# Linear attention whose weights and state are multiplied first, a Gram over 255 columns and ones, and another order of the drain and the late stage

## The chip, the cores and the metric

The kernel runs on one core of one Trainium2 chip. The metric is the device time in microseconds of one execution of the whole program. "Before" is the kernel as given, "after" is the changed one.

## The reference, cut to what matters

Four residual stages follow one another on x of 8 batches x 512 rows x 256 columns; `ln` is a layernorm over the 256 columns without gain or bias. The change is in the third, the attention without softmax:

```
x = x + ln(softmax_attention(ln(x)))          # 16 heads of 64, causal, with a slope bias
x = x + ln(linear_layer(ln(x)))
z  = ln(x)                                    # third stage
q  = z + z @ Wq + bq
k_i = z + z @ Wk[i] + bk[i]   (i = 0, 1)
v_i = z + z @ Wv[i] + bv[i]
state = prod_i (k_i^T v_i / 1024), per head of 16 columns
x = x + ln( (ln(q @ state) * ln_g + ln_b) @ Wo + bo )
x = x + ln( shared_ffn(ln(x)) + top8_of_64_experts(ln(x)) )
```

Neither kernel forms k and v. With the Gram matrix G = z^T z the state is A_k^T G A_v with A = I + W, and terms for the biases.

## The kernel before, in words

The five engines have one hand-ordered program each, coupled by semaphores. The program has four stretches.

**Attention stage** (about 0 to 1190 us of the trace). A batch is eight *steps*, one for each pair of heads; step g runs the scores of pair g and the transposes and value product of pair g-1. Batches 1 to 6 run in a loop, batch 0 ahead of it and batch 7 behind it. Steps run in the order 1 to 7, then 0. What TensorE does in a step is the tuple `TENSOR_STEP`: `P0`, `P1` are the two projections of the next pair (L1541), `S0`, `S1`, `S2` the three thirds of the scores (L1552), `Tsu` the transposes of the probabilities of head s, third u (L1564), `O` the value product (L1578). ScalarE's is `SCALAR_STEP` (`Esk` and `Fsk` are pieces of the exponentials, L798; `T`, `P`, `O` copy PSUM out, L781), VectorE's is `VECTOR_STEP` (`R0`, `R1`, `L2` add the bias and take the row minimum, L1081; `J` are reciprocals, L1090). GpSimd multiplies each head's probabilities by the reciprocals, four instructions a head (L675), and T00 waits for it.

The letters `b`, `q`, `k`, `e` (`A`, `B`, `C` on VectorE) are slots. The tables `TENSOR_AT`, `SCALAR_AT`, `VECTOR_AT`, `X_AT` and `RING_AT` put into a slot of a step the work of the *previous* batch p (everything behind its softmax attention), the norm of the following batch, and the value projections `V` 0 to 7 (L1532). Two PSUM banks, 4 and 5, form a ring through which P, V, T and O results pass in the order of issue; the ring's other users are `X`, `L` and, before only, `Q`.

Batch p's linear attention is a chain of parts: `x2_norm` writes z into `xn`; `gram` (L1630) forms G, with two extra columns of ones for the column sums; `L` (L1611) transposes z into `xTp`; `t1` (L1638) is G A_v; `state` is A_k^T t1 (L1646) and the sums' product with A_v (L1653); VectorE adds the bias terms and multiplies the two states into `sbd`, blocks of 16 on the diagonal; `Q` (L1616) forms the queries `qTp` from `xTp`; `rows` (L1661) multiplies them by `sbd`. Then follow `l1_sum`, `l1_norm`, `l1o_T`, `l1wo` (L1588) and so on.

**Drain and chain** (1180 to 1400 us). `drain` ends batch 7's softmax attention; `last_leave` (L1758) is its output projection over heads, into banks WO_BANK and WO_BANK + 1. It begins with

```
                pe.wait_ge(ring_ready, ring_count(a, ("O", HP - 2)))
                pe.wait_ge(biased, at(i, H * T, H * T))
                last_leave(range(HP - 2))
```

Batch 7's later parts then stand between *units* of the shared feed-forward of batches 0 to 4, in the order of the list `CHAIN` (`shared_hidden`, L1854, and every seventh unit `shared_out`, L1866).

**Experts** (1400 to 2064 us), L1951 and L1964. The change does not touch them.

**Late stage** (2064 us to the end). The shared feed-forward of batches 5 to 7 (n = 0, 1, 2), six hidden units f each, and meanwhile on VectorE the final norms of all batches. `shared_hidden` of unit f waits until VectorE's `gate` (L1364) of unit f-2 is done. `FINISH_AT` says behind which gate (n, f) VectorE does `sums` (statistics, L1004) and `scaled` (before: an inverse square root by eight small instructions, L1016 to L1031, and then the scaling, L1463) of which batch.

Of the kernel before, what the change touches and what calls it, by code (L numbers as in the profile page):

```python
# [39 lines left out]
ATT_STEPS, POST_STEPS = 17, 164  # L40
# [39 lines left out]
def bass_sandwich(nc, x, wq, wk, wv, wo, bo, ffn_w, ffn_d, l1_wq, l1_wqT, l1_bq, l1_wk, l1_bk, l1_wv, l1_bv,  # L80
# [12 lines left out]
    with ctx:  # L93
# [140 lines left out]
        gram_psum, gram_ready, ssum_ready = sem("gram_psum"), sem("gram_ready"), sem("ssum_ready")  # L234
# [47 lines left out]
        def score_banks(hp, u):  # L282
# [6 lines left out]
        TENSOR_AT = {(2, 'e'): ('ffn_T',), (3, 'q'): ('ffn',), (4, 'k'): ('gram',), (4, 'e'): ('t1',), (5,  # L289
                   'b'): ('state',), (6, 'q'): ('rows',), (7, 'b'): ('l1o_T',), (7, 'q'): ('l1wo',), (0,  # L290
                   'k'): ('moe_T',), (0, 'e'): ('logits',)}
        SCALAR_AT = {(2, 'e'): ('ffn_T',), (4, 'k'): ('gram',), (7, 'q'): ('l1o_T',), (0, 'k'): ('moe_T',), (0,
                   'e'): ('gates',)}
        VECTOR_AT = {(1, 'A'): ('wo_norm',), (1, 'B'): ('x1_sum',), (2, 'C'): ('x1_norm',), (3, 'B'): ('ffn_sum',
# [3 lines left out]
        X_AT = {(4, 'A'): 'means', (5, 'A'): 'rsqrt', (6, 'A'): 'scale'}  # L298


        RING_AT = {(1, 'b'): (('V', 4),), (2, 'q'): (('V', 5),), (4, 'b'): (('V', 6),), (4, 'q'): (('V', 7),), (5,
                   'b'): (('L', 0), ('L', 1)), (5, 'k'): (('Q', 0), ('Q', 1)), (6, 'k'): (('X', 0),), (7, 'b'): (('X',
                   1),), (7, 'e'): (('V', 0), ('V', 1)), (0, 'b'): (('V', 2),), (0, 'e'): (('V', 3),)}
# [105 lines left out]
        def t_unit(a, n):  # L409
# [7 lines left out]
                   'unit', 'unit', 'x1_sum', 'x1_norm', 'unit', 'unit', 'ffn_T', 'ffn', 'ffn_sum', 'ffn_norm', 'unit',  # L417
                   'x2_sum', 'x2_norm', 'unit', 'unit', 'gram', 'l1_T', 'unit', 't1', 'qp', 'unit', 'unit', 'state',
                   'unit', 'rows', 'l1_sum', 'l1_norm', 'unit', 'unit', 'l1o_T', 'unit', 'l1wo', 'unit', 'l1o_sum',
                   'unit', 'unit', 'l1o_norm', 'unit', 'unit', 'x3_sum', 'x3_norm', 'moe_T', 'logits', 'gates1',  # L420
                   'gates', 'gates2', 'unit', 'unit', 'rank', 'slots', 'unit', 'unit', 'unit']
# [1621 lines left out]
```

## Time and profile before

| | |
|---|---|
| median of 3 runs | 2169.01 us (2167.77 to 2172.38) |
| profiled execution, own time | 2168.89 us |
| profiled execution, span | 2166.8 us |
| TensorE busy | 2102.9 us, 97% |
| TensorE idle behind GpSimd's normalising | 27.1 us in 17 waits |
| chain that ended last | TensorE 83%, VectorE 7% |

The span is what the trace covers, 2.1 us less than the execution's own time. Busy time of TensorE is the union of its matmuls; each f32 matmul of the program appears as two instructions. "Idle before" is how long the engine stood still ahead of a group and which engine's instruction ended that.

### The profile page before, as it was taken

The numbers are of one execution on the slowest core, as the hardware profiler recorded it, in microseconds if no ns is written. First come the engines' busy times: TensorE is split into PE (matmuls) and PEld (weight loads), VectorE is DVE, ScalarE is ACT, GpSimd is POOL, SyncE is SP. The second block draws the span as 40 slices with busy tenths as digits, with TensorE's granted clock in tenths as the row PEclk, the third lists the DMA queues.
The fourth block names the chain that finished last, engine by engine and source line by source line (L and its number), as shares of the span: only waits on it lengthen the run. The fifth ranks groups of instructions, "written<-read, shape, count | busy, mean of one in ns | idle before, by whom it ended". The sixth has DMA issues, their size and how long they took to land.

```text
span 2166.8 us, 37485 instructions
## 1 busy us (share of the span) xinstructions
PE 2102.9 (97%) x11844; PEld 1550.7 (72%) x11844; DVE 975.6 (45%) x3780; ACT 828.7 (38%) x2130; POOL 842.5 (39%) x958
## 2 busy tenths in 40 slices
PE   8999999999999999999998999999999999999998
PEld 4555656566556656656565665799999999999956
DVE  3426655655565565575565534122222222222246
ACT  4746545645645555465465212111111111111110
POOL 3426526626446356266266230413232223222222
PEclk9999999999999999999999999999999999999999
DMA  9400001000000000000001300278778777888841
GB/s 319 121 0 11 11 22 64 35 30 25 25 18 21 35 16 5 31 17 6 20 22 58 139 28 35 70 264 270 257 259 272 269 260 257 268 262 270 270 109 59
DMA packets 101979, 245.43 MB, mean 113 GB/s; under 512 B 22916, under 2 KB 78435, under 8 KB 93488
## 3 DMA queue, kind: packets, MB, share of 16 engines
q1 hardware_dynamic: 75696, 223.83, 28.6%
q0 software_dynamic: 26112, 19.55, 5.5%
q8 instruction: 80, 1.31, 0.3%
q14 instruction: 91, 0.75, 0.1%
HBM read 193.71 MB, written 87.91 MB: 130 GB/s over the span
## 4 chain that ended last, share of the span: by engine, by line
PE 83%; DVE 7%; issue 4%; ACT 2%; POOL 2%; DMA 1%; DVEq 0%; POOLq 0%; ACTq 0%
PE bank L1951 19%; PE bank L1964 9%; PE bank L1541 9%; PE bank L1588 7%; PE bank L1854 6%; PE bank L1564 6%; PE bank L1578 5%; PE bank L1552 5%; PE bank L1866 3%; PE bank L1532 3%; POOL prob L675 2%; DVE stats L1004 2%; PE bank L1638 1%; PE bank L1616 1%; PE bank L1630 1%
## 5 line engine op out<-in xcount | busy, mean ns | idle before, releaser
L675 POOL TENSOR_TENSOR prob<-prob,rsum 128x128 f32<-128x128 f32 (+3 forms) x512 | 349.5, 715 | 541.6 <-DVE rsum L1090 541.5
L1951 PE MATMUL bank<-pT,big_w 128*128 128x160 f32 x3072 | 438.2, 299 | 0.0
L1951 PEld LDWEIGHTS bank<-pT,big_w 128*128 128x128 f32 x3072 | 422.7, 190 | 0.1
L680 POOL DMA_INDIRECT disp<-send,slot x288 | 285.4, 991 | 198.1 <-DVE slot L1284 109.5
L798 ACT ACTIVATE prob<-prob,negmax 128x512 f32<-128x512 f32 (+3 forms) x512 | 287.3, 568 | 80.6 <-DVE negmax L1081 80.1
L726 POOL DMA_INDIRECT acc<-qk,token_e x64 | 99.1, 1549 | 490.1 <-issue 171.4
L1081 DVE CUSTOM_DVE_ANT_0 prob<-bank,bias 128x512 f32<-128x512 f32 (+3 forms) x512 | 220.7, 487 | 109.7 <-PE bank L1552 100.5
L1541 PE MATMUL bank<-xT,big_w 128*128 128x512 f32 x512 | 250.9, 614 | 6.4 <-ACT v_s L781 3.5
L956 ACT ACTIVATE pT<-bank 128x480 f32<-128x480 f32 x128 | 73.1, 571 | 458.7 <-PE bank L1951 458.7
L1410 DVE TENSOR_TENSOR pT<-pT,bank 128x480 f32<-128x480 f32 x128 | 83.8, 655 | 335.9 <-PE bank L1951 335.8
L1964 PE MATMUL bank<-pT,big_w 128*128 128x160 f32 x1536 | 219.3, 299 | 0.0
L781 ACT ACTIVATE pT<-bank 128x512 f32<-128x512 f32 (+1 forms) x384 | 182.6, 538 | 90.5 <-PE bank L1564 90.3
L1564 PEld LDWEIGHTS bank<-ident,prob 128*128 128x128 f32 x1280 | 145.3, 142 | 99.4 <-issue 60.8
L1964 PEld LDWEIGHTS bank<-pT,big_w 128*128 128x128 f32 x1536 | 210.6, 190 | 0.0
L1564 PE MATMUL bank<-ident,prob 128*128 128x128 f32 x1280 | 177.6, 278 | 27.9 <-POOL prob L675 27.1
L1552 PE MATMUL bank<-qk 64*128 64x512 f32 (+3 forms) x1024 | 173.2, 456 | 0.0
L1552 PEld LDWEIGHTS bank<-qk 64*128 64x128 f32 x1024 | 87.9, 186 | 106.6 <-issue 85.2
L1541 PEld LDWEIGHTS bank<-xT,big_w 128*128 128x128 f32 x512 | 91.2, 193 | 94.1 <-issue 81.0
L1578 PE MATMUL bank<-pT,v_s 128*64 128x512 f32 (+3 forms) x1024 | 152.0, 439 | 0.7 <-ACT pT L781 0.6
L781 ACT ACTIVATE v_s<-bank 128x512 f32<-128x512 f32 x74 | 44.2, 597 | 253.3 <-PE bank L1532 194.0
L1532 PE MATMUL bank<-big_w,xT 128*128 128x512 f32 x256 | 121.5, 608 | 0.1
L1578 PEld LDWEIGHTS bank<-pT,v_s 128*64 128x64 f32 x1024 | 65.4, 136 | 75.5 <-issue 62.9
(197 smaller groups left out, 2501.5 us busy)
## 6 DMA issues: line engine op xcount, KB each, us to landing
big_w<-ew SPq DMA_DIRECT2D x64, 1536.0 KB, 6.9
big_w<-ew SPq DMA_DIRECT2D x64, 768.0 KB, 5.9
disp<-send SPq DMA_DIRECT2D x1, 10272.0 KB, 37.4
xT<-disp SPq DMA_DIRECT2D x64, 160.5 KB, 5.4
disp<-send,slot POOLq DMA_INDIRECT x288
x<-x SPq DMA_DIRECT2D x8, 512.0 KB, 4.0
x_d<-x SPq DMA_DIRECT2D x8, 512.0 KB, 2.7
hT_d<-hT SPq DMA_DIRECT2D x8, 512.0 KB, 2.6
```

What stands on the lines that cost most here:

```text
L675: i = g.tensor_tensor(pr, pr, rsum[:, n, t:t + 1].to_broadcast([P, COLS[t]]), ALU.mult)
L680: g.indirect_dma_start(out=disp, out_offset=bass.IndirectOffsetOnAxis(ap=slot[:, t, k:k + 1], axis=0), in_=send[:, t, :], in_offset=None, ...
L781: return a.activation(dst, src, ACT.Copy)
L798: a.activation(prob[:, n % 4, at_t], prob[:, n % 4, at_t], ACT.Exp, bias=negmax[:, n, t:t + 1], scale=-1.0, accum_out=psumm[:, n, t:t + 1] ...
L1081: v.tensor_tensor_reduce(out=prob[:, n % 4, P_AT[t]:P_AT[t] + COLS[t]], in0=bank[score_banks(hp, u)[s]][:, col:col + COLS[t]], in1=bias[:, ...
L1532: ins = mm(ring_bank(a, key)[:], xT[:, c, m % T * P:(m % T + 1) * P], wv_s[:, c, m // T * 512:(m // T + 1) * 512], start=(c == 0), stop=(c ...
L1541: ins = mm(ring_bank(a, key)[:], w[:, c, hp * P:(hp + 1) * P], xT[:, c], start=(c == 0), stop=(c == C - 1))
L1552: ins = mm(bank[score_banks(hp, u)[s]][:, col:col + COLS[t]], qT[half, hp % 2, t * P:(t + 1) * P], kT[half, hp % 2, 0:COLS[t]], start=True ...
L1564: ins = nc.tensor.transpose(ring_bank(a, key)[:, col + (t - j) * P:col + (t - j + 1) * P], prob[:, n % 4, P_AT[t] + j * P:P_AT[t] + (j + 1 ...
L1578: ins = mm(dst[s * DH:(s + 1) * DH, j * P:N], v_s[:, j, (2 * hp + s) * DH:(2 * hp + s + 1) * DH], pT[:, s, T_AT[j]:T_AT[j] + N - j * P], s ...
L1951: i = mm(bank[2 * half + 1 - part][:, q * CAP:(q + 1) * CAP], w1[:, c, f * P:(f + 1) * P], xbT[:, c], start=(c == 0), stop=(c == C - 1), s ...
L1964: i = mm(bank[(4, 7)[c]][:, 0:CAP], w2[:, f, c * P:(c + 1) * P], act_e[:, f], start=(f == 0), stop=(f == FC - 1), skip_group_check=True)
```

## The change

1. **Order of the products.** The `Q` units, `qTp`, and the product of the sums with A_v are gone. A new part `fuse` multiplies A_q (loaded transposed) by `sbd` into a 256 x 256 matrix `fused`, ScalarE copies it out, and `rows` multiplies `xTp` by it.
2. **255 columns and ones.** The rows of z sum to zero, so column 0 is dropped: the Gram, the transposes and A_q read `xn` from column 1 on, and column 256, which holds ones, takes its place. The biases become the last row or column of the A matrices (more, smaller DMAs at the start, and some subtractions once in batch 0 on VectorE). The bias terms on VectorE in `t1` and `state` fall away; ScalarE copies `t1` out instead.
3. **Drain.** `WO_BANK` is 0 instead of 2, the wait is for all but the last two bias results, and in batch 7's step 7 VectorE does the last third of the last pair ahead of `x3_norm`.
4. **Orders.** All slot tables, `TENSOR_STEP`, `SCALAR_STEP`, `CHAIN` and `FINISH_AT` are new, and the inverse root is a part of its own, `roots`.

```
-        WO_BANK = 2
+        WO_BANK = 0
-            return RING_BANKS[0] if (i[1], f) == (0, 1) else 2 * (f % 2)
+            return RING_BANKS[0] if (i[1], f) == (0, 1) else 2 * ((f + (i[1] < EARLY)) % 2)
-        TENSOR_STEP = ('b', 'P0', 'S0', 'S1', 'q', 'T00', 'P1', 'T01', 'T02', 'T10', 'T11', 'S2', 'T12', 'k', 'O', 'e')
-        SCALAR_STEP = ('b', 'F03', 'F13', 'P0', 'q', 'E00', 'T00', 'E01', 'P1', 'T01', 'T02', 'T10', 'T11', 'E02', 'T12',
-                       'E10', 'E11', 'k', 'O', 'e', 'E12')
+        TENSOR_STEP = ('P0', 'b', 'S0', 'S1', 'q', 'T00', 'P1', 'T01', 'T02', 'T10', 'T11', 'k', 'T12', 'S2', 'O', 'e')
+        SCALAR_STEP = ('F03', 'F13', 'P0', 'b', 'q', 'E00', 'T00', 'E01', 'P1', 'T01', 'T02', 'T10', 'T11', 'k', 'E02',
+                       'E10', 'T12', 'E11', 'E12', 'O', 'e')
...
-                     (1, 0): [("scaled", 1)], (1, 1): [("sums", EARLY)], (1, 2): [("scaled", EARLY)],
+        FINISH_AT = {(0, 5): [("sums", 0), ("roots", 0)], (1, 0): [("scaled", 0), ("sums", 1)],
...
-                    for c in range(C):
-                        a.activation(ssum_b[:, c], ones_f[:], ACT.Copy,
-                                     scale=gram[:, c, D:D + 1]).then_inc(ssum_ready, 1)
+                elif part == "t1":
+                    for k in range(KS):
+                        act.wait_ge(t1_psum, at(p, KS, k + 1))
+                        a_copy(t1[:, k].rearrange("p c d -> p (c d)"), bank[PA + k][:]).then_inc(t1_ready, 1)
+                elif part == "fuse":
+                    act.wait_ge(fused_psum, at(p, 1, 1))
+                    a_copy(fused[:].rearrange("p c d -> p (c d)"), bank[PB][:]).then_inc(fused_ready, 1)
...
+                    if part == "B" and a[0] is None and a[1] == B - 1 and g == HP - 1:
+                        last_pair()
...
-                            ins = mm(bank[PA + c][:, 0:D + 2], xn[:, t, c * P:(c + 1) * P], xn[:, t, 0:D + 2],
+                            ins = mm(bank[PA + c][:, 0:D], xn[:, t, c * P + 1:(c + 1) * P + 1], xn[:, t, 1:D + 1],
...
-                            ins = mm(bank[PB][:, k * D:(k + 1) * D], ssum_b[:, c], a_v[:, k, c], start=(c == 0),
-                                     stop=(c == C - 1), skip_group_check=True)
+                elif part == "fuse":
+
+                    pe.wait_ge(sbd_ready, at(p, 1, 1))
+                    for h in range(C):
                         for c in range(C):
+                            ins = mm(bank[PB][:, h * D + c * P:h * D + (c + 1) * P],
+                                     a_q[:, c, h * P + 1:(h + 1) * P + 1], sbd[:, c], start=True, stop=True,
+                                     skip_group_check=True)
+                    ins.then_inc(fused_psum, 1)
                 elif part == "rows":
+                    pe.wait_ge(fused_ready, at(p, 1, 1))
+                    rows_out(xTp, lambda c: fused[:, c], C, rows_psum)
...
-                pe.wait_ge(biased, at(i, H * T, H * T))
+                pe.wait_ge(biased, at(i, H * T, H * T - 2))
```

Of the new slot tables three entries matter below: V7 stands at (4, 'k') and not at (4, 'q'), V5 at (2, 'b') and not at (2, 'q'), and `moe_T` at (0, 'q') and not at (0, 'k').

**TensorE, batch 7, end of step 3 to step 4's first projections** (the loop has the same order). Before, L1578 is O, L1532 are V6 and V7, L1541 P0 and P1, L1552 S0 and S1, L1564 T00:

```order
L1578 MATMUL bank4<-pT,v_s 64x256 x2
L1532 MATMUL bank5<-big_w,xT 128x512 x2
L1541 MATMUL bank4<-xT,big_w 128x512 x2
L1552 MATMUL bank0<-qk 128x512
L1552 MATMUL bank1<-qk 128x512
L1552 MATMUL bank2<-qk 128x384
L1552 MATMUL bank3<-qk 128x384
L1552 MATMUL bank2<-qk 128x128
L1552 MATMUL bank3<-qk 128x128
L1532 MATMUL bank5<-big_w,xT 128x512 x2
L1564 MATMUL bank4<-ident,prob 128x128 x4
L1541 MATMUL bank5<-xT,big_w 128x512 x2
```

The same place after; lines 1570, 1524, 1533, 1544 and 1556 are the 1578, 1532, 1541, 1552 and 1564 of before:

```order
L1570 MATMUL bank4<-pT,v_s 64x256 x2
L1533 MATMUL bank5<-xT,big_w 128x512 x2
L1524 MATMUL bank4<-big_w,xT 128x512 x2
L1544 MATMUL bank0<-qk 128x512
L1544 MATMUL bank1<-qk 128x512
L1544 MATMUL bank2<-qk 128x384
L1544 MATMUL bank3<-qk 128x384
L1544 MATMUL bank2<-qk 128x128
L1544 MATMUL bank3<-qk 128x128
L1556 MATMUL bank5<-ident,prob 128x128 x4
L1533 MATMUL bank4<-xT,big_w 128x512 x2
```

P0 and V6 have changed places, and V7 no longer stands between the scores and T00; it comes seven rows later, between T11 and T12.

**VectorE, batch 7, around the last pair's last third** (L1081 on banks 2 and 3, then the reciprocals). Before, from batch 6's last residual sum on:

```order
L1028 SCALAR_TENSOR_TENSOR newton1<-newton1,vare1 128x4
L1031 SCALAR_TENSOR_TENSOR rstd1<-newton1,rstd1 128x4
L1112 TENSOR_SCALAR send<-x2,mv1,rstd1 128x256 x4
L1081 ISA prob,negmax<-bank2,bias 128x256
L1081 ISA negmax 128x1
L1081 ISA prob,negmax<-bank3,bias 128x256
L1081 ISA negmax 128x1
L1090 RECIPROCAL rsum<-psumm 128x4 x2
L1134 TENSOR_TENSOR y<-bank2,bo_b 128x512
L1134 TENSOR_TENSOR y<-bank3,bo_b 128x512
```

And after:

```order
L1198 TENSOR_TENSOR x2<-x2,y 128x1024
L996 BN_STATS stats1<-x2 128x6 x4
L1000 BN_AGGR mv1<-stats1 128x2 x4
L1002 TENSOR_SCALAR vare1<-mv1 128x4
L1073 ISA prob,negmax<-bank2,bias 128x256
L1073 ISA negmax 128x1
L1073 ISA prob,negmax<-bank3,bias 128x256
L1073 ISA negmax 128x1
L1082 RECIPROCAL rsum<-psumm 128x4 x2
L1008 TENSOR_SCALAR rstd1<-vare1 128x4
L1010 TENSOR_TENSOR newton1<-rstd1 128x4
```

The last third has moved ahead of the inverse root and the scaling of `x3_norm`; the output projection is read from banks 0 and 1.

## Rows read from the trace of the kernel before

**Rows 1.** The page's part 1, TensorE: busy us, share of the span, instructions.

```profile
PE 2102.9 (97%) x11844; PEld 1550.7 (72%) x11844; DVE 975.6 (45%) x3780; ACT 828.7 (38%) x2130; POOL 842.5 (39%) x958
```

**Rows 2.** Waits of TensorE: who for whom, us in total, times, longest.

```profile
PE bank L1564 <- POOL prob L675: 27.1, 17, 2.9
PE bank L1758 <- DVE negmax L1081: 7.4, 1, 7.4
...
PE bank L1541 <- ACT v_s L781: 3.5, 14, 0.3
```

**Rows 3.** Groups by line and shape, TensorE: busy us, mean ns, idle before.

```profile
L1588 PE MATMUL bank<-l1wo_s,xTp 128*128 128x256 f32 x128 | 29.7, 385 | 0.1
...
L1616 PE MATMUL bank<-xTp,a_q 128*128 128x512 f32 x64 | 29.5, 604 | 0.0
L1630 PE MATMUL bank<-xn 128*128 128x258 f32 x128 | 29.2, 381 | 0.0
...
L1661 PE MATMUL bank<-sbd,qTp 128*128 128x128 f32 x128 | 16.3, 281 | 0.0
...
L1653 PE MATMUL bank<-a_v,ssum_b 128*128 128x256 f32 x64 | 15.1, 380 | 0.0
...
L1601 PE MATMUL bank<-ident,send 128*128 128x128 f32 x64 | 8.3, 274 | 0.0
L1611 PE MATMUL bank<-ident,xn 128*128 128x128 f32 x64 | 8.3, 273 | 0.0
```

**Rows 4.** Timeline of TensorE, a loop batch, step 4: start us, us, instruction.

```profile
503.69 1.98 PE L1532 MATMUL bank<-big_w,xT 128*128 128x512 f32 x4
...
509.25 1.98 PE L1532 MATMUL bank<-big_w,xT 128*128 128x512 f32 x4
```

**Rows 5.** Timeline of VectorE and of GpSimd, the same batch.

```profile
496.81 1.43 DVE L1004 BATCH_NORM_STATS2 stats<-bank 128x6 f32<-128x256 f32 x4 [1.67 <-PE bank L1588]
...
507.83 5.46 POOL L675 TENSOR_TENSOR prob<-prob,rsum 128x128 f32<-128x128 f32 x8 [3.03 <-DVE rsum L1090]
```

**Rows 6.** Timeline of TensorE, the same batch, step 0, with its idle time.

```profile
584.51 0.65 PE L1564 MATMUL bank<-ident,prob 128*128 128x128 f32 x4 [0.90 <-POOL prob L675]
```

**Rows 7.** Timelines of TensorE and VectorE at the drain.

```profile
1177.11 2.37 PE L1578 MATMUL bank<-pT,v_s 128*64 128x512 f32 x16 [0.56 <-ACT pT L781]
1186.90 12.57 PE L1758 MATMUL bank<-big_w,oT 128*128 128x256 f32 x48 [7.42 <-DVE negmax L1081]
...
1182.89 0.17 DVE L1010 TENSOR_SCALAR vare<-mv 128x4 f32<-128x4 f32 x1
```

**Rows 8.** Stretches: busy us (instructions) of the five engines, granted clock, DMA, GB/s.

```profile
86.00:100.00 14.00, 12.49 (x70) 7.14 (x68) 6.96 (x28) 9.34 (x26) 7.42 (x12) 1.00 0.00 0
...
466.30:470.00 3.70, 3.70 (x10) 1.81 (x11) 3.42 (x13) 1.22 (x4) 2.58 (x4) 0.63 0.00 0
...
619.40:623.00 3.60, 3.60 (x21) 2.59 (x22) 3.35 (x12) 2.38 (x6) 2.58 (x4) 1.00 0.00 0
...
1186.90:1191.00 4.10, 4.10 (x10) 3.30 (x11) 0.35 (x2) 0.64 (x4) 3.50 (x6) 0.51 0.02 4
```

**Rows 9.** Timelines of VectorE and TensorE in the late stage, n = 1.

```profile
2093.92 1.41 DVE L1004 BATCH_NORM_STATS2 stats<-big_w 128x6 f32<-128x256 f32 x4 [11.43 <-DMA big_w<-acc]
...
2097.68 1.38 DVE L1463 TENSOR_SCALAR big_w<-big_w,mv,rstd 128x256 f32<-128x256 f32 x4
...
2105.62 1.27 DVE L1450 TENSOR_TENSOR big_w<-big_w,bank 128x512 f32<-128x512 f32 x2
2091.89 7.03 PE L1854 MATMUL bank<-xa,prob 128*128 128x512 f32 x16
2102.29 15.66 PE L1854 MATMUL bank<-xa,prob 128*128 128x512 f32 x32 [3.37 <-DVE oT L1364]
```

**Rows 10.** Timelines of ScalarE and TensorE, the same loop batch, end of step 3.

```profile
501.54 0.41 ACT L781 ACTIVATE pT<-bank 128x256 f32<-128x256 f32 x1
501.81 0.76 ACT L798 ACTIVATE prob<-prob,negmax 128x512 f32<-128x512 f32 x1
...
501.39 2.37 PE L1578 MATMUL bank<-pT,v_s 128*64 128x512 f32 x16
```

More of the change, by code:

```diff
@@ L39 @@
 WARM = 16
-ATT_STEPS, POST_STEPS = 17, 164
+ATT_STEPS, POST_STEPS = 17, 159
 RSQRT_GUESS = float(0x5F3759DF)
@@ L286, in bass_sandwich @@
         SENDS = -(-T * TOPK // (HP - 2))
[L289 to L294, printed above, removed]
[3 rows of a table removed]
@@ L298, in bass_sandwich @@
[L298 to L303, printed above, removed]
+        TENSOR_AT = {(2, 'e'): ('ffn_T',), (3, 'q'): ('ffn',), (4, 'e'): ('gram',), (5, 'b'): ('t1',), (5,
+                   'q'): ('state',), (5, 'k'): ('fuse',), (6, 'q'): ('rows',), (6, 'e'): ('l1o_T',), (7,
+                   'q'): ('l1wo',), (0, 'q'): ('moe_T',), (0, 'e'): ('logits',)}
@@ new lines, in bass_sandwich @@
+        SCALAR_AT = {(2, 'e'): ('ffn_T',), (4, 'e'): ('gram',), (5, 'q'): ('t1',), (6, 'b'): ('fuse',), (6,
+                   'e'): ('l1o_T',), (0, 'q'): ('moe_T',), (0, 'e'): ('gates',)}
+        VECTOR_AT = {(1, 'B'): ('wo_norm', 'x1_sum'), (2, 'A'): ('x1_norm',), (3, 'B'): ('ffn_sum', 'ffn_norm',
+                   'x2_sum'), (4, 'B'): ('x2_norm',), (5, 'B'): ('state',), (6, 'B'): ('l1_sum',), (6,
+                   'C'): ('l1_norm',), (7, 'A'): ('l1o_sum', 'l1o_norm', 'x3_sum'), (7, 'B'): ('x3_norm',), (0,
+                   'B'): ('gates1', 'gates2', 'slots')}
@@ L319, in ring_units @@
             units = RING_AT.get((g, slot), ())
-            return [u for u in units if (post or u[0] not in "LQ") and
+            return [u for u in units if (post or u[0] != "L") and
                     (following or not (u[0] == "X" or u[0] == "V" and u[1] < T))]
@@ L416, in bass_sandwich @@
         CHAIN = ["logits'", 'wo_sum', "gates1'", "gates'", "gates2'", 'unit', 'unit', "rank'", "slots'", 'wo_norm',
[L417 to L421, printed above, removed]
+                   'unit', 'unit', 'x1_sum', 'x1_norm', 'unit', 'unit', 'ffn_T', 'ffn', 'ffn_sum', 'ffn_norm',
+                   'x2_sum', 'x2_norm', 'unit', 'unit', 'gram', 'unit', 'l1_T', 'unit', 't1', 'unit', 'state', 'unit',
+                   'unit', 'fuse', 'rows', 'l1_sum', 'l1_norm', 'unit', 'unit', 'l1o_T', 'unit', 'l1wo', 'unit',
+                   'unit', 'l1o_sum', 'unit', 'unit', 'l1o_norm', 'unit', 'x3_sum', 'x3_norm', 'moe_T', 'logits',
+                   'gates1', 'gates', 'gates2', 'unit', 'unit', 'rank', 'slots', 'unit', 'unit', 'unit', 'unit',
+                   'unit']
         CHAIN_L1 = CHAIN[:CHAIN.index("l1_T")].count("unit")
-        assert CHAIN_L1 > FC and CHAIN_L1 // (FC + 1) == CHAIN[:CHAIN.index("qp")].count("unit") // (FC + 1)
+        assert CHAIN_L1 > FC
         CHAIN += ["unit"] * (len(steps) - CHAIN.count("unit"))
@@ L943, in _ @@
                         a_copy(xTp[:, c], bank[4 + c][:]).then_inc(l1T_ready, 1)
-                elif part == "qp":
-                    for c in range(C):
-                        act.wait_ge(qp_psum, c + 1)
-                        a.activation(qTp[:, c], bank[4 + c][:], ACT.Identity, bias=bq_c[:, c:c + 1]
-                                     ).then_inc(qp_ready, 1)
                 else:
@@ L1292, in extras, with last_pair @@
                     x_norm(following, X_AT[g, at_slot])
+            def last_pair():
+                bias_round(last, HP - 1, 2)
+                for n in (H - 2, H - 1):
+                    reciprocals(last, n)
             def step(a, g, p, following):
@@ L1482, in _ @@
                             sums(b)
+                        elif what == "roots":
+                            roots()
                         else:
```

135 lines of the change are left out of this document (49 added, 86 removed), and 3 rows, old and new, of the table VECTOR_AT.

## The prediction, written before the run

> **What bounds the kernel now.** I read first how busy the engines are: TensorE 97% of the span, no other over 45% [rows 1]. So a microsecond of matmul taken away is a microsecond gained, unless TensorE then waits. Second, TensorE's waits: 27.1 us behind GpSimd's normalising (17 times, at T00), 7.4 once at the drain, 3.5 in 14 short ones behind copies of V [rows 2]. Together with start and tail these are its 64 us of idle time (2166.8 - 2102.9). Third, the groups by shape, for what each part of the linear attention costs [rows 3]. Last, the timelines of the places where the new order moves something: the reader is to see there when an operand is ready and when TensorE would want it.
>
> **1. Products.** Per program, from the busy time of their groups [rows 3]: the queries go, -29.5; the sums' product with A_v goes, -15.1; rows by diagonal blocks (128 columns) go, -16.3; rows by the full `fused` matrix come, which are as many products of 128x256 as `l1wo` has, +29.7; `fuse` is half as many products of 128x128 as rows had, +8.2. The Gram loses 2 of 258 columns of 29.2: -0.2. Sum -23.2. These busy times count the pipelined end of each group, some 0.1 us, and per batch three groups go and two come, so I take **-22.4**. All of it is on TensorE, thus on the path. ScalarE gets two copies of t1 and one of `fused` and loses two of `qTp` and the `ssum_b` pair; VectorE loses its bias terms; both stay far below TensorE. The work of a few subtractions on VectorE and ten DMAs more is once, in batch 0, where VectorE waits for TensorE: 0.
>
> The operands that now start at column 1 cost nothing by the trace: `send` has rows of 321 elements, so three of its four tiles start off a 16-byte boundary, and its transposes take 274 ns against 273 for `xn`, whose rows of 260 elements start on one [rows 3]. The Trainium skill (SBUF — State Buffer, Door 1: The DMA port swizzle, the note on cachelines) speaks against the change: SBUF has 16-byte lines, and each access that goes on to a new line pays. As an estimate by that page, 33 lines instead of 32 for 128 columns would add a thirty-second to Gram, transposes and `fuse`, 1.4 us; the trace does not agree for transposes, and shows nothing of a Gram so placed.
>
> **2. Drain.** O ends at 1179.48, and L1758 stands idle until 1186.90, because the last bias third is queued on VectorE behind `x3_norm` [rows 7]. After, that product needs only what was done at step 7, and bank 0; what is late next is ScalarE's copy of O, which I put at 0.7 (a pass over 512 columns takes 0.76 at most [rows 10]). So 6.7 of 7.4 go. The first 4.1 us behind the wait ran at a granted clock of 0.51, the lower of the two levels (1.2 of 2.4 GHz) [rows 8]: 48 instructions took 12.57 where the rate of L1588 gives 11.1. That is 1.5 more: **-8.2**. T00 after those 11 us, at 1191, finds its probabilities: the last pair now follows `x3_sum`, which ended at 1183.06 [rows 7], and needs some 4.5 more. The bound the other way is 0, if another wait held it to 1186.9.
>
> **3. Late stage.** At n = 1, TensorE waits 3.37 us for the gate that is queued behind sums 0, roots, scaling 0 and sums 1; the four units behind it then take 15.66 where two take 7.03, which is 1.9 too many [rows 9], again the lower clock. After, only sums 0 and roots 0 precede the gate: 3.76 us (2093.92 to 2097.68), and the gate is done at 2098.4, before TensorE wants it at 2098.8. But the work comes later: I replayed the new list with sums 2.2, roots 1.6, scaling 1.4 and 1.3 more for batches 5 and 6 [rows 9], gates 0.7 and a unit of 3.4. It gives waits of 0.5, 0.2, 0.8 and 0.2 in n = 1 (start of n = 2 3.5 earlier), then 0.9 and 0.9 in n = 2, where batch 6's sums and roots now stand at its fourth and fifth gate. Net **-1.8**; bounds -5.3 (none of the new waits) and +1.
>
> **4. Attention steps.** V5 and V7 leave the slot ahead of T00 and P1, where the ring's bank was not yet copied out: the 14 waits go, **-3.5** [rows 2]. In step 0 `moe_T` (8.3 / 8 = 1.0 us [rows 3]) moves ahead of T00, into a wait of 0.90 [rows 6]; its two copies delay ScalarE's next ones, so I take 0.6 of it in 6 batches: **-3.6**.
>
> V7's move has a price too. In step 4 the first head is normalised at 507.83 + 5.46 / 2 = 510.6 [rows 5]. This is set by VectorE, which starts `ffn_sum` when `ffn` is done (496.81) and goes through to the residual sum before the last pair's third; nothing in that changes. TensorE has done its scores at 509.25, and fills the time with V7 (1.8 us) [rows 4]. After, V7 comes later and T00 stands there: a new wait of 1.3 us, in 7 batches **+9.2**. Bounds: 0 and 1.8 per batch.
>
> The wait of 2.3 us in step 1, behind batch end's `wo_sum`, keeps its 5.6 us of cover (V4 stays ahead of T00): 0.
>
> In batch 0 light steps wait for F03, which ScalarE did behind O's copy and the short exponential E12; E12 now goes ahead of O. At half of the 0.76 of a wide one [rows 10] and four such waits: **-1.5**.
>
> **5. Chain.** `fuse` and `rows` stand next to each other, so TensorE waits for a copy, +0.7; `x3_norm` has one unit less of cover ahead of `moe_T`, +0.6: **+1.3**.
>
> **Sum.** -22.4 - 8.2 - 1.8 - 3.5 - 3.6 + 9.2 - 1.5 + 1.3 = -30.5. Against the profiled execution's own 2168.9, that is 2138.4; the median of the three runs is 2169.0, so I say **2138**.
>
> **Rivals.**
> - *The lower clock follows the new waits.* After step 1's wait of about the same length in each batch the granted clock fell in some (0.63 over 3.7 us at 466) and not in others (1.00 at 619) [rows 8]. Each fall costs 3.7 x 0.37 = 1.4 us. If step 4's waits do this too: 7 x 1.4 = +10, 2148. Against it: none of the waits of 0.9 to 1.5 us did, as between 86 and 100 [rows 8]. 17%.
> - *Step 4's wait does not appear,* since VectorE or GpSimd is earlier than I think: -9, 2129. For it: GpSimd's sends and VectorE's small instructions share the time in ways I have only from one order. 16%.
> - *Slower: ScalarE's queue holds up every O.* After, E10 (0.76) goes ahead of T12's copy, which O's last product needs. O starts at 501.39, and its last 256 of 1280 columns begin 1.9 us later, at 503.2; T12's copy, 0.7 later than before, is done at 502.7 [rows 10]. If that 0.5 us of slack is not there, each of the 63 pairs waits. From 0.5 us each on, the whole gain is gone; with 0.6, +38 - 31: 2176. 4%.
> - *Slower: operands at column 1 run at half speed.* Gram 29.2, transposes 8.3, `fuse` 8.2 once more [rows 3]: +45.7, 2184. The transposes of `send` speak against it. 2%.
> - The rest, 61%, is the forecast, with 2131 to 2145 as its own range: the drain and late terms within their bounds, and one more or less fall of the clock in step 1, whose place against the rest of the program shifts.
>
> **How the numbers follow.** The range takes in the first two rivals and a little of their own spread: 2127 to 2150. A change of less than 0.2% (4.3 us) could not be told from none here. Faster than that: forecast and the first two rivals, less a few in a hundred for what I don't see, 0.92; slower 0.05, the last two rivals rounded down for their mild cases; the same 0.03.
>
> **What would show it.** Right: TensorE's busy time near 2080; L1758's wait under 1 us; a wait of about 1.3 at T00 in step 4 of each batch and none in step 0; in the late stage several waits under 1 us instead of one of 3.4; a batch in the loop about 2.7 + 0.7 - 1.3 = 2 us shorter. Wrong: waits of L1578 behind ScalarE's pT in every step; Gram products over 400 ns; waits in step 5 or 6, where t1, state and `fuse` now follow one another through ScalarE and VectorE with 2 to 4 us of cover each.

## The result, and the profile after

The changed kernel takes 2119.0 us (median of 4 runs, 2117.2 to 2120.2) where the kernel before takes 2168.6 beside it: the ratio is 0.9764, 95% interval 0.9748 to 0.9779. The forecast of 2138 had the direction right and most of its terms, but it was 19 us too high and its range (2127 to 2150) did not hold the time.

The page's part 1 for TensorE, and the span with the mean granted clock of the kernel after:

```profile
PE 2060.5 (97%) x11780; PEld 1538.2 (73%) x11780; DVE 952.1 (45%) x3719; ACT 825.1 (39%) x2122; POOL 841.8 (40%) x958
...
core 0: 2116.9 us, clock 0.999
```

Beside [rows 1], the busy time is 42.4 us shorter, and the idle time went from 64 to 56 us. The span is 49.9 us shorter. So nearly all of the gain stands in busy time, and the products alone can't fill it: they were to give 22 to 24.

The groups of TensorE by shape, which answer to [rows 3]:

```profile
L1556 PE MATMUL bank<-ident,prob 128*128 128x128 f32 x1280 | 169.7, 275 | 20.5 <-POOL prob L672 19.9 <-ACT pT L778 0.5
...
L1580 PE MATMUL bank<-fused,xTp 128*128 128x256 f32 x128 | 29.7, 386 | 0.8 <-ACT fused L778 0.8
...
L1617 PE MATMUL bank<-xn 128*128 128x256 f32 x128 | 29.0, 379 | 0.0
...
L1593 PE MATMUL bank<-ident,send 128*128 128x128 f32 x64 | 8.7, 279 | 0.0
L1642 PE MATMUL bank<-sbd,a_q 128*128 128x128 f32 x64 | 8.5, 275 | 0.0
```

The new `rows` cost the 29.7 and `fuse` 8.5 (8.2 was taken). The Gram that starts at column 1 takes 379 ns a product where 258 columns took 381: no price for the shifted start. The transposes of the probabilities, whose number is unchanged, were busy 177.6 us before and 169.7 now, but that is mostly a matter of counting: behind P1 they used to be two groups, busy 1.69 and 0.44 us, and are now one of 1.91 in most steps; b_s2_last below has 165.3 and no shorter time. The first hint of where the rest came from is in the projections, as many as before, which follow the wait at T00. Before, then after:

```profile
L1541 PE MATMUL bank<-xT,big_w 128*128 128x512 f32 x512 | 250.9, 614 | 6.4 <-ACT v_s L781 3.5 <-ACT xT L781 2.1 <-DVE xT L1312 0.9
...
L1533 PE MATMUL bank<-xT,big_w 128*128 128x512 f32 x512 | 246.2, 604 | 0.9 <-DVE xT L1295 0.9
```

They are 10 ns each shorter. b_v4_split below, which has of the change only V4's new place and no fall of the clock in the loop, shows 605.

The waits of TensorE, which answer to [rows 2]:

```profile
PE bank L1556 <- POOL prob L672: 19.9, 25, 2.2
PE bank L1544 <- DVE negmax L1073: 8.6, 7, 1.4
...
PE bank L1515 <- ACT pT L778: 3.4, 7, 0.6
PE bank L1832 <- DVE oT L1351: 1.9, 2, 1.1
```

The reader is to see that 17 waits for GpSimd with a total of 27.1 have become 25 with a total of 19.9, and that a kind of wait stands there that the kernel before did not have inside the scores: 7 times, 1.2 us each, for VectorE's minimum. Step 1 has much of both: T00 waited 15.6 us there in seven batches before, and waits 3.0 after, beside the 8.6 inside the scores. (At T00 of step 4 seven new waits, 9.7 in all, have come, as forecast.) The timeline of step 1, TensorE, in a loop batch after:

```profile
744.44 1.13 PE L1544 MATMUL bank<-qk 64*128 64x512 f32 x4
746.81 1.14 PE L1544 MATMUL bank<-qk 64*128 64x384 f32 x8 [1.24 <-DVE negmax L1073]
747.88 1.98 PE L1524 MATMUL bank<-big_w,xT 128*128 128x512 f32 x4
750.28 0.65 PE L1556 MATMUL bank<-ident,prob 128*128 128x128 f32 x4 [0.42 <-POOL prob L672]
```

and the stretches around it (busy us of the engines, then granted clock, DMA, GB/s):

```profile
744.00:748.00 4.00, 2.76 (x15) 1.11 (x14) 2.73 (x15) 1.55 (x5) 0.60 (x2) 1.00 0.00 0
748.00:752.00 4.00, 3.58 (x11) 1.62 (x12) 3.93 (x15) 2.21 (x6) 4.00 (x7) 1.00 0.00 0
```

Before, the same place was one wait of 2.1 to 2.4 us at T00, and behind it the granted clock fell in four of the six loop batches (0.63 over the stretch of 3.7 us from 466.3 in [rows 8]). Now V4 (L1524) stands behind the scores and parts the wait in two, 1.24 and 0.42, and the clock stays at 1.00 behind it in every batch.

Where the 49.9 us lie, from the starts of the first score product of batch 1, of batch 7, of O ahead of the drain, of the first expert product and of the first product behind the experts (157.33, 1072.62, 1177.11, 1399.32, 2060.43 before; 154.79, 1039.10, 1141.89, 1352.92, 2014.02 after) and the two spans:

| stretch | before | after | change | forecast |
|---|---|---|---|---|
| start and batch 0 | 157.3 | 154.8 | -2.5 | -2.0 |
| six loop batches | 915.3 | 884.3 | -31.0 | -15.1 |
| batch 7, steps | 104.5 | 102.8 | -1.7 | -1.9 |
| drain and chain | 222.2 | 211.0 | -11.2 | -9.7 |
| experts | 661.1 | 661.1 | 0.0 | 0 |
| late stage | 106.4 | 102.9 | -3.5 | -1.8 |

Four fifths of the miss is in the loop. A loop batch of before is 151.4 and 151.6 us long where the clock holds and 152.8 to 153.4 where it falls; after, all six are 147.2 to 147.5.

### The profile page after: what moved, and what is told of

Read it like the earlier page. It is cut to its first block, busy times and chain, and to the rows that moved or that the text cites. A ratio compares the mean times of both kernels' runs of the same rounds, so it can differ in the third digit from the quotient of the medians.

```text
span 2116.9 us, 37253 instructions
## 1 busy us (share of the span) xinstructions
PE 2060.5 (97%) x11780; PEld 1538.2 (73%) x11780; DVE 952.1 (45%) x3719; ACT 825.1 (39%) x2122; POOL 841.8 (40%) x958
## 4 chain that ended last, share of the span: by engine, by line
PE 82%; DVE 8%; issue 4%; ACT 3%; POOL 2%; DMA 1%; DVEq 0%; SPq 0%; POOLq 0%; ACTq 0%
PE bank L1925 20%; PE bank L1938 10%; PE bank L1580 8%; PE bank L1533 7%; PE bank L1832 6%; PE bank L1570 6%; PE bank L1544 5%; PE bank L1556 5%; PE bank L1844 4%; PE bank L1524 4%; DVE stats L996 2%; POOL prob L672 2%; PE bank L1617 1%; PE bank L1625 1%; ACT pT L778 1%
## 5 line engine op out<-in xcount | busy, mean ns | idle before, releaser
L1533 PE MATMUL bank<-xT,big_w 128*128 128x512 f32 x512 | 246.2, 604 | 0.9 <-DVE xT L1295 0.9
L1556 PEld LDWEIGHTS bank<-ident,prob 128*128 128x128 f32 x1280 | 146.5, 141 | 80.3 <-issue 60.9
L1556 PE MATMUL bank<-ident,prob 128*128 128x128 f32 x1280 | 169.7, 275 | 20.5 <-POOL prob L672 19.9
L1570 PE MATMUL bank<-pT,v_s 128*64 128x512 f32 (+3 forms) x1024 | 152.0, 439 | 2.2
L1570 PEld LDWEIGHTS bank<-pT,v_s 128*64 128x64 f32 x1024 | 64.8, 136 | 83.2 <-issue 52.3
L1524 PE MATMUL bank<-big_w,xT 128*128 128x512 f32 x256 | 120.1, 597 | 0.6 <-DMA big_w<-wv 0.6
L1580 PE MATMUL bank<-big_w,oT 128*128 128x256 f32 x448 | 99.9, 382 | 5.8 <-DVE key L1246 5.1
```

Source lines behind the costliest of these rows:

```text
L1524: ins = mm(ring_bank(a, key)[:], xT[:, c, m % T * P:(m % T + 1) * P], wv_s[:, c, m // T * 512:(m // T + 1) * 512], start=(c == 0), stop=(c ...
L1533: ins = mm(ring_bank(a, key)[:], w[:, c, hp * P:(hp + 1) * P], xT[:, c], start=(c == 0), stop=(c == C - 1))
L1556: ins = nc.tensor.transpose(ring_bank(a, key)[:, col + (t - j) * P:col + (t - j + 1) * P], prob[:, n % 4, P_AT[t] + j * P:P_AT[t] + (j + 1 ...
L1570: ins = mm(dst[s * DH:(s + 1) * DH, j * P:N], v_s[:, j, (2 * hp + s) * DH:(2 * hp + s + 1) * DH], pT[:, s, T_AT[j]:T_AT[j] + N - j * P], s ...
L1580: ins = mm(bank[PA + t // 2][:, (t % 2) * D:(t % 2 + 1) * D], lhs[:, c, t * P:(t + 1) * P], rhs(c), start=(c == 0), stop=(c == chunks - 1) ...
```

## The experiments

Eleven more kernels were timed, each with its ratio to the kernel before. A *batch* below is the mean length of the loop batches in which the clock does not fall, from the first scores of step 1 to the next; *falls* counts the seven step 1s (batches 1 to 7) behind whose wait the granted clock fell. Both are read from one execution of each kernel, and the number of falls can differ in another: p_only took 2141.3 to 2148.0 us at mean granted clocks of 0.996 to 0.992, and its 5 falls are those of the longest execution.

| kernel | ratio, 95% interval | batch, us | falls |
|---|---|---|---|
| before | 1 | 151.5 | 4 |
| after | 0.9764 (0.9748 to 0.9779) | 147.4 | 0 |
| b_s2_last | 0.9996 (0.9987 to 1.0005) | 151.4 | 4 |
| b_v4_split | 0.9965 (0.9952 to 0.9979) | 151.4 | 0 |
| b_drain | 0.9954 (0.9941 to 0.9968) | 151.4 | 4 |
| b_late | 0.9991 (0.9982 to 1.0000) | 151.6 | 4 |
| p_only | 0.9875 (0.9856 to 0.9894) | 148.2 | 5 |
| a_v7_q | 0.9741 (0.9728 to 0.9754) | 146.5 | 0 |
| a_v4_front | 0.9769 (0.9755 to 0.9783) | 147.3 | 2 |
| a_moe_k | 0.9794 (0.9780 to 0.9807) | 148.6 | 0 |
| a_late_old | 0.9760 (0.9746 to 0.9773) | 147.4 | 0 |
| a_best | 0.9777 (0.9764 to 0.9791) | 148.1 | 0 |
| b_v4_late | 1.0099 (1.0084 to 1.0115) | none | 7 |

**Is it the wait of step 1, and its being in one piece, that lowers the clock?** First the kernel before with nothing but V4 moved:

```
-        RING_AT = {(1, 'b'): (('V', 4),), (2, 'q'): ...
+        RING_AT = {(1, 'q'): (('V', 4),), (2, 'q'): ...
```

> The kernel before, with one edit: V4 of step 1 stands behind S0 and S1 and no longer ahead of P0. Theory (clock): the one wait of 2.1 to 2.3 us at T00 of step 1 becomes two shorter ones, about 1.2 inside the scores (VectorE's minimum of the bank's last holder) and 0.4 to 0.9 at T00, and the granted clock falls in no loop batch; all batches take 151.0 to 151.6 and the program 5 to 8 us less: 2161 to 2164. Rival 1 (the split alone doesn't hold the clock up; it is the shorter sum of the waits or another place): falls stay in 3 or 4 batches, 2167 to 2170. Rival 2: the wait isn't split at all, T00 still stands 2.1 us.

Step 1 of a loop batch, TensorE:

```profile
763.38 1.13 PE L1552 MATMUL bank<-qk 64*128 64x512 f32 x4
765.98 1.14 PE L1552 MATMUL bank<-qk 64*128 64x384 f32 x8 [1.48 <-DVE negmax L1081]
767.05 1.98 PE L1532 MATMUL bank<-big_w,xT 128*128 128x512 f32 x4
769.45 0.65 PE L1564 MATMUL bank<-ident,prob 128*128 128x128 f32 x4 [0.42 <-POOL prob L675]
```

The wait is split as in the kernel after, no batch has a fall, they are 151.0 to 151.7, and the six loop batches together are 6.9 us shorter (908.4 for 915.3). The batch itself gained nothing (151.4 for 151.5), though the two waits together are 1.6 to 2.0 us where the one was 2.1 and 2.4 in the undisturbed batches before. In time it is 0.35% (0.21 to 0.48), 7.6 us. The wait is split and the falls are gone, so both rivals are out as they were put; that it was the smaller sum of the waits, and not the cut between them, isn't.

Then the reverse, the kernel after with V4 ahead of the scores again:

```
-        RING_AT = {(1, 'q'): (('V', 4),), (2, 'b'): ...
+        RING_AT = {(1, 'b'): (('V', 4),), (2, 'b'): ...
```

> The kernel after with one edit: V4 of step 1 ahead of S0, not behind S1, so that step 1's two waits (1.24 and 0.42) become one at T00. Theory (clock): one wait of 1.7 to 2.3 us; the sum of waits changes by less than 0.5 a batch; if such a wait is long enough for the chip to lower the clock, 3 to 6 of the loop batches take 1.6 us more and the program 5 to 10 more than after, 2124 to 2129. Rival (falls hang on something else that the new orders changed): no falls, 2117 to 2121, every batch within 0.5 of 147.4.

Step 1 of batches 3 and 4, TensorE, and the clock behind the two waits:

```profile
454.26 0.65 PE L1556 MATMUL bank<-ident,prob 128*128 128x128 f32 x4 [2.33 <-POOL prob L672]
...
602.67 0.65 PE L1556 MATMUL bank<-ident,prob 128*128 128x128 f32 x4 [1.96 <-POOL prob L672]
...
454.00:458.00 4.00, 3.74 (x9) 1.72 (x10) 3.72 (x13) 1.19 (x3) 2.84 (x5) 0.63 0.00 0
602.70:606.70 4.00, 4.00 (x24) 2.84 (x24) 3.73 (x14) 2.81 (x7) 2.55 (x4) 1.00 0.00 0
```

One wait stands there again, 1.9 to 2.3 us, and the clock falls behind two of seven; those batches are 148.8 and 148.5, 1.2 to 1.5 longer than the others. That is the sign of the theory, at fewer places than I gave it (3 to 6). The time, 2120.6 us, lies in the rival's range, and the ratio can't be told from that of after. Last, the kernel before with V4 (`'k'` for `'b'`) behind T12, so that nothing covers the wait:

> The kernel before with V4 of step 1 neither ahead of P0 nor ahead of T00, but behind T12. So nothing covers the wait for GpSimd: about 1.2 to 1.5 us inside the scores and 2.2 more at T00, with only half a dozen score products between. Theory (the clock falls after the longer waits, more often the longer they are): a fall in 5 to 7 of the 7 places, an undisturbed batch 153.0 to 153.4, one with a fall 154.7 to 155.2; the program 12 to 18 us more than before, 2181 to 2187. Rival (a wait of 2 us or of 3.7 in two parts makes no difference; falls in 3 or 4 places): 2178 to 2181.

```profile
783.31 1.14 PE L1552 MATMUL bank<-qk 64*128 64x384 f32 x8 [1.55 <-DVE negmax L1081]
786.78 1.11 PE L1564 MATMUL bank<-ident,prob 128*128 128x128 f32 x4 [2.33 <-POOL prob L675]
...
785.00:792.00 7.00, 5.22 (x13) 3.03 (x14) 6.60 (x25) 2.60 (x6) 4.37 (x6) 0.51 0.00 0
```

Now the clock falls in all seven, and in four of them it stays down about twice as long, as in these 7 us at 0.51. The loop batches are 154.4 to 156.2, the program 0.99% slower (0.84 to 1.15), 21 us, more than the 12 to 18 expected. So the clock follows TensorE's waits in step 1. Parted by V4 into 0.8 to 1.5 and 0.4, the wait had no fall behind it in 42 places (six kernels); in one piece of 1.9 to 2.4 it had one in 23 of 42 (the other six); with 1.2 to 1.5 and then 2.3 inside 5 us, in 7 of 7. These runs don't tell whether the cut between the two waits counts or their smaller sum. The parted waits add up to 1.3 to 2.0 us, mostly less than the one piece, and two waits that add up to 3.5 to 3.9 had a fall each time although there is a cut between them. At about the same sum, 1.89 to 1.99, five parted ones had no fall, and two of four in one piece had one, which is too few to decide. Within the one-piece waits length does not decide: one of 1.93 had a fall, in p_only, and one of 2.36 in batch 1 of the kernel before had none; in the late stage a wait of 3.37 had a fall behind it in the kernel before and none in a_late_old. The Trainium skill (TensorE: Matmul & The Clock Gate, The HAM clock gate) says that the monitor's window runs freely and is not reset when a kernel starts; by that, the same wait would have a fall at some phases and none at others, which is what these counts look like. No run here shifted the phase on purpose. The kernel after has one fall ahead of the loop, behind a wait of 2.21 us in batch 0 (0.57 from 36 to 40 us), where the kernel before waited 2.89 with none.

**How much is the products?** The products, columns and copies of after under the step orders, slot tables, drain and late stage of before. The core of the edit: `TENSOR_AT` as it then stands, and the change to `RING_AT` of before:

```
+        TENSOR_AT = {..., (4, 'e'): ('t1',), (5, 'b'): ('state',), (6, 'b'): ('fuse',), (6, 'q'): ('rows',), ...
-                   'b'): (('L', 0), ('L', 1)), (5, 'k'): (('Q', 0), ('Q', 1)), ...
+                   'b'): (('L', 0), ('L', 1)), ...
```

> The products, the 255 columns and ones and their copies as in after, but the step orders, all slot tables, the drain and the late stage of before; the two Q units are simply left out, t1 is copied by ScalarE in step 4, fuse stands at the head of step 6 ahead of rows. Theory 1 (the extra gain of the loop lies in the orders): an undisturbed loop batch takes 151.4 - 2.8 - 0.1 = 148.5 us, with a fall of the clock 150.1; the program 2169 less 22 to 24, 2145 to 2147. Theory 2 (it lies in the products, since two groups fewer also means fewer changes from one kind of matmul to another): undisturbed batch 147.0 to 147.5, program 2134 to 2138. A new wait at fuse or rows, behind VectorE's product of the states, would show as up to 1 us a batch the other way.

A batch takes 148.1 and 148.3, so the products give about 3.3 a batch, 0.5 more than the forecast's 2.8 and near theory 1; the rest down to after's 147.4 is the orders'. The program is 27 us faster (23 to 31 by the interval), with one fall more than before. The waits are those of before, which shows that the products alone leave the pattern as it was:

```profile
PE bank L1544 <- POOL prob L670: 26.3, 17, 2.9
PE bank L1724 <- DVE negmax L1071: 7.5, 1, 7.5
```

**How much are the orders?** From p_only to after the fourth batch goes from 148.3 to 147.3, and step by step: steps 1 and 2 lose 0.5 (V4, 1.8 us of it, counted where it now stands), step 0 loses 0.8, steps 3 and 7 together 0.2, steps 4 to 6 gain 0.5. Three of the moves were undone or done alone.

The transposes T12 ahead of S2, in the kernel before:

```
-        TENSOR_STEP = (..., 'T11', 'S2', 'T12', 'k', 'O', 'e')
+        TENSOR_STEP = (..., 'T11', 'T12', 'S2', 'k', 'O', 'e')
```

> The kernel before, with one edit: in TENSOR_STEP T12 stands ahead of S2, not behind it. In the traces of both kernels the stretch T10 to T12 and S2 takes 2.62 us a step before (T 1.62, S2 0.63, T12 0.37) and 2.47 to 2.59 after. Theory (order of kinds): TensorE loses time at each change from scores to transposes and back, so an undisturbed loop batch falls from 151.4 us by 0.3 to 0.8, and the whole program by 2 to 6: 2163 to 2167. Rival (the order of kinds costs nothing; the part of the gain that products and waits don't explain is all the clock): 2168 to 2170, a batch of 151.4.

It gains 0.1 a batch and nothing that can be measured. The sixteen transposes behind P1 get 0.15 shorter a step (1.84 for 1.62 and 0.37), but S2 ahead of O takes 0.75 in place of 0.63. The rival holds here.

V7 back in its old slot, in the kernel after (`(4, 'q')` for `(4, 'k')`):

> The kernel after with one edit: V7 back in step 4's slot between the scores and T00. Prediction's term (the moved V7 uncovers 1.3 us at T00 of step 4): the wait of 1.45 us there goes, about 0.3 comes back at P1 behind the copy of V7, and a batch takes 146.2 to 146.5 instead of 147.4; the program 7 to 8 us less than after, 2111 to 2113. Rival (V7 only moves with what follows: GpSimd is late in the steps behind, so that the wait comes back in step 5 or behind T12): 2117 to 2120.

Step 4 of a loop batch in after, and then in this kernel:

```profile
789.40 2.00 PE L1544 MATMUL bank<-qk 64*128 64x512 f32 x12
792.85 0.65 PE L1556 MATMUL bank<-ident,prob 128*128 128x128 f32 x4 [1.45 <-POOL prob L672]
```

```profile
786.13 1.99 PE L1524 MATMUL bank<-big_w,xT 128*128 128x512 f32 x4
787.95 0.60 PE L1556 MATMUL bank<-ident,prob 128*128 128x128 f32 x4
788.80 1.98 PE L1533 MATMUL bank<-xT,big_w 128*128 128x512 f32 x4 [0.25 <-ACT v_s L778]
```

The wait of 1.45 goes and 0.25 comes back at P1, as expected; the batch gains 0.85 and not 1.2, since V7, P1 and S2 each take 0.1 longer from start to start in their new company. The program takes 2115.1 us, 2 more than the range expected, a ratio of 0.9741 beside after's 0.9764; the intervals overlap, but every loop batch of the trace is 0.3 to 1.2 shorter. This is the fastest median of all the kernels here.

`moe_T` back behind the transposes, in the kernel after (`(0, 'k')` for `(0, 'q')` on TensorE and ScalarE):

> The kernel after with one edit: moe_T of step 0 back in the slot behind T12, on TensorE and ScalarE. Prediction's term: with it ahead of T00 0.6 us a batch is gained; the traces of both orders show step 0 0.8 shorter. So step 0's wait of 0.9 at T00 comes back, a batch takes 148.0 to 148.3 instead of 147.4, the program 4 to 6 us more than after, 2123 to 2125. If one or more falls of the clock come with it, up to 2128. Rival (step 0 gained by something else, as V4's move to step 1): a batch within 0.3 of 147.4, 2118 to 2120.

```profile
719.23 0.65 PE L1556 MATMUL bank<-ident,prob 128*128 128x128 f32 x4 [1.04 <-POOL prob L672]
...
726.95 2.37 PE L1570 MATMUL bank<-pT,v_s 128*64 128x512 f32 x16 [0.38 <-ACT v_s L778]
```

The wait at T00 is back, and O waits for the copy of V3 behind it: 1.3 a batch, 0.3% of the time, more than the 0.6 to 0.9 expected. Since `'k'` stands between T11 and T12 in the new order and behind T12 in the old one, this is not quite the step of the change; between p_only and after step 0 shows 0.8.

A try at something faster, a_v7_q with X1 moved behind O, away from X0:

> The kernel after with V7 back ahead of T00 in step 4, and the second transpose unit X1 of step 6 behind O instead of next to X0. V7 alone gave 2115.1. The wait of 0.47 us at X1 (the ring's bank not yet copied out) goes if the copy is the cause: a batch 146.0 instead of 146.5, the program 2111 to 2113. Rival (the copy of X1 is then late for P0 of step 7, or O waits behind X0): 2114 to 2118.

```profile
835.14 0.44 PE L1556 MATMUL bank<-ident,prob 128*128 128x128 f32 x2 [0.47 <-ACT pT L778]
...
841.27 1.98 PE L1533 MATMUL bank<-xT,big_w 128*128 128x512 f32 x4 [1.30 <-ACT xT L778]
```

The wait of 0.47 only goes on to T12, and P0 of step 7 now stands 1.30 us for the copy of X1. The rival was right, and more than in its numbers: 1.5 a batch lost against a_v7_q.

**The drain alone**, in the kernel before: `WO_BANK` 0, `H * T - 2`, `last_pair` and the swapped hidden banks, as in the diff of the change.

> The kernel before with the drain of after alone: WO_BANK 0, the wait for all but two bias results, the last pair's last third on VectorE ahead of x3_norm in step 7 of batch 7, and the banks of the first hidden units swapped. Prediction's step: wait of 7.4 down to 0.7 and 1.5 of clock, 8.2 in all, 2161. The pair of traces shows 9.4 (wait gone altogether, 10.63 in place of 12.57 us behind it): 2159 to 2160. Rival: in the kernel before, VectorE is later at step 7 than in after, the wait stays 1 to 4 us or comes back at T00 of the last pair: 2162 to 2167.

```profile
1178.17 2.38 PE L1583 MATMUL bank<-pT,v_s 128*64 128x512 f32 x16 [0.54 <-ACT pT L781]
1180.48 10.63 PE L1763 MATMUL bank<-big_w,oT 128*128 128x256 f32 x48
```

The projection follows O with no wait at all, and takes 10.63 in place of 12.57 [rows 7]; the ratio is 0.46% (0.32 to 0.59), 10 us. The kernel after has the same two rows:

```profile
1141.89 2.37 PE L1570 MATMUL bank<-pT,v_s 128*64 128x512 f32 x16
1144.19 10.63 PE L1736 MATMUL bank<-big_w,oT 128*128 128x256 f32 x48
```

**The late order alone**, in the kernel before (`FINISH_AT` and `roots` of the change), and the old one in the kernel after, with `("roots", b)` put ahead of each `("scaled", b)` of the table of before:

> The kernel before with the new FINISH_AT and the inverse root as a part of its own, nothing else. Prediction's step: 1.8 us less (bounds 5.3 less and 1 more), 2167. The pair of traces shows the late stage 3.5 us shorter, which gives 2165 to 2166 if it is this edit alone. Rival: the late stage gains in after since the drain's new banks or the phase of the clock give it a stretch without a fall; then within 1 us of 2168.6.

> The kernel after with the late order of before (scaling ahead of the gate, sums 1 behind gate 5 of n = 0). From the expert's last product to the end it was 100.7 us before, 99.3 with the new order alone, 99.5 with the old order and the new drain, 97.2 after; and batch 0's row sums on VectorE started 34.4, 35.1, 33.2 and 32.4 us behind the experts. Theory (two parts: the order gives 2.0, the rest is how early the accumulated rows of batch 0 land): 2.0 us more if they land as in after, 99.2; 1 us either way with the landing; program 2120 to 2122. Rival (the order gives all 3.5): 100.5 to 101, 2122.5.

The late stage of after, TensorE, with its waits, and batch 0's row sums on VectorE:

```profile
2090.24 2.85 PE L1832 MATMUL bank<-y,prob 128*128 128x384 f32 x8 [0.74 <-DVE oT L1351]
2093.67 8.01 PE L1844 MATMUL bank<-prob,oT 128*128 128x256 f32 x36 [0.58 <-DVE oT L1351]
...
2045.44 1.41 DVE L996 BATCH_NORM_STATS2 stats<-big_w 128x6 f32<-128x256 f32 x4 [9.36 <-DMA big_w<-acc]
```

and of a_late_old:

```profile
2055.28 7.18 PE L1832 MATMUL bank<-xa,prob 128*128 128x512 f32 x16 [3.37 <-DVE oT L1351]
...
2046.92 1.41 DVE L996 BATCH_NORM_STATS2 stats<-big_w 128x6 f32<-128x256 f32 x4 [11.44 <-DMA big_w<-acc]
```

From the end of the experts' last product to TensorE's last it takes 100.8 us before, 99.4 in b_late, 99.6 in b_drain, 97.3 after and 100.1 in a_late_old. The row sums start when batch 0's accumulated rows have landed, which was 34.1, 34.8, 32.9, 32.1 and 34.1 us behind the experts. With the old order, 1.2 us earlier (before to b_drain) was worth 1.2. By that b_late, had its rows landed 0.6 earlier, as in the kernel before, would stand at 98.7 where the old order has 100.1 (a_late_old, no fall of the clock there) or 100.8 (before, with one): the new order gives 1.4 to 2.0. The other 1.5, from 98.7 to 97.3, came with a landing 2.1 us earlier. The traces of the other kernels put the order by itself a little lower, where no fall of the clock stands in the stage: with the new one and rows at 34.0 and 34.1 a_moe_k and a_v7_q take 98.9, 1.2 less than a_late_old; with the old one and rows at 32.4 b_v4_split takes 98.2, 0.9 more than after. Why the rows land at other times from one kernel to the next was not tried. In whole times neither order can be told from the other: b_late is 0.09% (0.00 to 0.18), and a_late_old's 0.9760 is after's 0.9764.

## Why the prediction was wrong

The step that failed is the sentence on step 1: "The wait of 2.3 us in step 1, behind batch end's `wo_sum`, keeps its 5.6 us of cover (V4 stays ahead of T00): 0." V4 does stay ahead of T00, but it no longer stands ahead of the scores. S1 meets VectorE's minimum on the way, so the wait is parted, and the clock stops falling. I had read in [rows 8] that the clock falls behind this wait in some batches and priced a fall at 1.4, but only as something that new waits might add. That all of those there could go was in no term and no rival; the forecast's own range had one fall more or less. In the loop this is 6 to 7 us: b_v4_split shows it with V4's move alone, and 4 x 1.6 is what the disturbed batches of before are longer. With it the sum would have been some 2131 or 2132, in the range; it is the largest of the errors and not the only one that took the time out of the range. And its size is in part luck: the kernel after with V4 back in front (a_v4_front) has two falls and not four, and its six loop batches are 2.3 us longer, not 6.5. Whether the parting of the wait or its smaller sum keeps the clock up stays open.

The others, term by term:

- *Products, -22.4.* Right in kind, 0.5 a batch too small: p_only shows 3.3 a batch for 2.8, some 26 in all. 0.2 of the 0.5 is a wait of P1 behind ScalarE's copy of `xT`, which the kernel before has in each loop batch and p_only has not; where the rest lies was not tried.
- *Operands at column 1.* They cost nothing that shows: 379 ns for the Gram. The transposes of `xn` take 273 ns in p_only, from column 1 in the old order, as in [rows 3] from column 0. After, they take 279, but so do those of `send`, which read the same columns in both kernels (274 before), so such a difference comes from the neighbours in the order; there is no 1.4 us to be seen.
- *Drain, -8.2.* 9.4. The mechanism was right, the 0.7 for ScalarE's copy did not come (the projection over the first pairs doesn't need it), and the lower clock had cost 1.9, not 1.5.
- *Late stage, -1.8.* The order gave 0.9 to 2.0 by the pairs with like landings, but the stretch is 3.5 shorter, with the landing of batch 0's rows as the part that I had taken for fixed. There are no waits in n = 1, where I had four, and 0.7 and 0.6 in n = 2.
- *V5 and V7 at P1, -3.5.* The waits went. With step 1's they are the 0.5 a batch of steps 1 and 2. But two kinds of wait came that no term had: 0.4 at T00 of step 2 in the six loop batches, and 0.5 at the transposes X1 of step 6, behind ScalarE's copy (3.4 in seven, L1515 above). I had named waits in step 6 as a sign of being wrong.
- *`moe_T`, -3.6.* 0.8 a batch by step 0 of p_only and after, not 0.6.
- *V7, +9.2.* The wait of 1.3 came as worked out: 1.4 in the loop batches, 1.2 in batch 7. But undoing the move is worth 0.85 a batch and not 1.3. I had added the lost cover and the ring's wait as if nothing else in the step changed.
- *Light steps, -1.5, and chain, +1.3.* In batch 0 the waits at T00 are 0.2 to 0.7 shorter each, and `rows` waits 0.8 for the copy of `fused`, as said; drain and chain without the drain's 9.4 gained 1.8 for 1.5.

Two readings were off as well. The idle time beyond the three waits named was not only start and tail: other waits, 5.1 us in six behind VectorE's `key` and 4.5 in two behind its `gate` among them, are some 17 of the 64 us. And the batch that was to be 2 us shorter is 2.6 by the terms themselves (2.8 + 0.5 + 0.6 - 1.3); an undisturbed one was 4.1 shorter. TensorE's busy time is 2060.5 and not 2080, of which about 7 is the counting of the transposes.

So of the 19 us, about 6.5 are the clock in step 1, 4 the products, 1.7 the late stage and 1.2 the drain, and the 6 that are left lie with the orders of the steps: 3 of them the term on V7 (0.45 in seven batches), 1 `moe_T`, the rest small pieces that had no term. The sizes of the small pieces in steps 3 to 7 rest on the pair of traces, not on a run of their own.

As to the rivals: step 4's new waits did not lower the clock (1.00 throughout), they were not absent, ScalarE's queue held up no O (2.2 us of idle time before all of L1570), and no operand ran at half speed. What I should have had as a rival is the mirror of the first one: that falls which stood in the kernel before would go.

## What to carry to other kernels

Where TensorE is the bound, look up behind which waits the granted clock is low, and treat "this wait is broken up or made smaller" as a term of its own: here moving one unit of 1.8 us by a few places, with an undisturbed batch as long as before, gave 0.35%. When an order is changed, go through it for every unit that now stands on the other side of a possible wait, not only for those whose slot name changed. And add up what a moved filler covers where it leaves and where it lands from a run with the move alone: by the timeline it was 1.3 here, by the run 0.85.

## What the runs showed of the hardware that I had not expected

- Waits of only 1.9 to 2.4 us in an otherwise full TensorE are followed by a fall to 0.5 of the clock in 23 of 42 places, and in 0 of 42 when the wait comes in two pieces of 0.8 to 1.5 and 0.4 us, which together are mostly shorter.
- Two waits close together (1.2 to 1.5 and 2.3) are worse than one of 2.3: 7 of 7, four of them with 7 us at 0.51 or so.
- The same wait of 3.37 us in the late stage was followed by a fall in the kernel before and by none in a_late_old.
- Sixteen transposes and S2 take about the same time in either order (2.59 and 2.62 us), since most of what the transposes win S2 ahead of O loses.
